# Full-height score products, a row tensor loaded by quarters, and a separate fine order of two streams for each engine

## The reference

```
q = (x @ Wq + bq).reshape(b, h, dh, t)        # likewise k, v; h = 16, dh = 8, t = 512
attn = jnp.einsum('bhdt,bhds->bhts', k, v) * temperature
attn = jax.nn.softmax(attn, axis=-1)
out = jnp.einsum('bhdt,bhts->bhds', q, attn)
...
h = shift_token(x)
q, k, v = jnp.split(h @ wqkv, 3, axis=-1)     # 8 heads of 64
q = l2norm(q) * qs ; k = l2norm(k) * ksc
q, k = rotary_xpos(q, k)                      # t*cos + rotate_half(t)*sin
x = x + local_attention(q, k, v) @ wo
h = layernorm(shift_token(x)) * lg + lb
a, g = split(h @ w1 + b1) ; x = x + (a * gelu(g)) @ w2 + b2
```

## Time and profile before

| | us |
|---|---|
| median of three executions | 1737.1 |
| profiled execution (its span) | 1743.6 (1741.7) |
| stage one with its start-up, to the last residual | 0 to 631 |
| stage two | 631 to 1741.7 |

### The profile page before, as it was taken

One profiled execution on the slowest core, in us unless ns is written; L12 is line 12 of the kernel. 1 busy time (PEld: TensorE's weight loads), 2 busy tenths in 40 slices (PEclk: granted clock), 3 DMA queues, 4 the chain that ended last, 5 costly groups with the idle time before them and its releaser, 6 DMA issues. The chain is left out here.

```text
span 1741.7 us, 21308 instructions
## 1 busy us (share of the span) xinstructions
PE 1380.9 (79%) x6968; PEld 733.4 (42%) x6968; DVE 1046.6 (60%) x2065; ACT 955.9 (55%) x2810; POOL 506.9 (29%) x525
## 2 busy tenths in 40 slices
PE   3898999989998976677686687687766877777876
PEld 3333333333332325445454454364444554544544
DVE  6665655666566666555556646657556566556563
ACT  0575655666576754555555465464555654545654
POOL 2000000000000024453443533624534525336241
PEclk9555555565555568898888898988988988889889
DMA  6212020211202000000011000010000010100010
GB/s 212 80 69 95 3 97 1 97 50 48 97 0 97 1 1 22 10 13 22 1 28 28 1 22 22 1 29 19 9 22 7 16 28 1 28 22 1 22 28 7
DMA packets 24157, 58.98 MB, mean 34 GB/s; under 512 B 2352, under 2 KB 2544, under 8 KB 22896
## 3 DMA queue, kind: packets, MB, share of 16 engines
q1 hardware_dynamic: 24048, 57.62, 10.9%
HBM read 23.98 MB, written 18.87 MB: 25 GB/s over the span
## 5 line engine op out<-in xcount | busy, mean ns | idle before, releaser
L530 ACT ACTIVATE E<-slot,neg_max 128x512 f32<-128x512 f32 x512 | 345.2, 686 | 229.7 <-DVE neg_max L804 125.8
L804 DVE TENSOR_REDUCE neg_max<-slot 128x2 f32<-128x1024 f32 x256 | 308.4, 1213 | 135.2 <-PE slot L1061 135.0
L1061 PE MATMUL slot<-v_rows,k_rows 32*128 32x512 f32 x512 | 269.3, 671 | 59.0 <-ACT E L530 47.3
L466 POOL TENSOR_TENSOR rot_work<-rot_work,rz 128x512 f32<-128x512 f32 x128 | 135.0, 1055 | 545.1 <-DVE rz L881 545.1
L589 ACT ACTIVATE rot_work<-bank,neg 128x128 f32<-128x128 f32 x512 | 180.8, 366 | 190.1 <-issue 119.0
L1061 PEld LDWEIGHTS slot<-v_rows,k_rows 32*128 32x128 f32 x512 | 132.1, 306 | 309.8 <-issue 174.6
L1071 PE MATMUL o_bank<-E,qz 128*32 128x512 f32 x1024 | 241.0, 1035 | 0.2 <-POOL qz L438 0.2
L1111 PE MATMUL bank<-wqkv_sb,hs 128*128 128x512 f32 x384 | 212.7, 670 | 14.3 <-ACT hs L556 13.6
L438 POOL TENSOR_TENSOR qz<-qT,rz 128x32 f32<-128x32 f32 x128 | 30.6, 239 | 586.3 <-DVE rz L808 586.3
L453 POOL TENSOR_TENSOR work<-work,rot_work 128x512 f32<-128x512 f32 x128 | 162.5, 1270 | 39.3 <-DVE rot_work L843 34.3
L1130 PEld LDWEIGHTS bank<-kT,q_bd 128*128 128x128 f32 x1024 | 142.1, 201 | 33.3 <-issue 28.7
(11 more groups left out here) (124 smaller groups left out, 1989.8 us busy)
## 6 DMA issues: line engine op xcount, KB each, us to landing
k_rows<-k_scr SPq DMA_DIRECT2D x8, 1024.0 KB, 5.7
v_rows<-v_scr SPq DMA_DIRECT2D x8, 1024.0 KB, 7.9
work<-v_al SPq DMA_DIRECT2D x16, 512.0 KB, 4.4
work<-v_al SPq DMA_DIRECT2D x16, 384.0 KB, 5.7
k_scr<-hi SPq DMA_DIRECT2D x16, 256.0 KB, 3.0
k_scr<-lo SPq DMA_DIRECT2D x16, 256.0 KB, 3.4
v_scr<-hi SPq DMA_DIRECT2D x16, 256.0 KB, 3.1
v_scr<-lo SPq DMA_DIRECT2D x16, 256.0 KB, 3.4
```

Source lines behind the costliest of these rows:

```text
L466: pool.tensor_tensor(pr[s][:, u % PR_SLOTS], pr[s][:, u % PR_SLOTS], rz2[s][:, u, :].unsqueeze(2).broadcast_to([P, 4, 2 * W]), ALU.mult).t ...
L530: last = act.activation(E[:, g % E_RING, 2 * half + m, :], slot[:, m], ACT.Exp, bias=neg_max[:, n, m:m + 1], accum_out=z[:, n, m:m + 1])
L804: dve.tensor_reduce(neg_max[:, n, :], slot[:], AX.X, ALU.max, negate=True).then_inc(max_ready, 1)
L1061: last = pe.matmul(slot[:, m], k_rows[32 * hh:32 * hh + 32, par, q, P * j:P * (j + 1)], v_rows[32 * hh:32 * hh + 32, par, q, :], start=Tru ...
```

## The change

Stage one: the score products use all 128 rows. `k_rows` is now zeroed once by POOL and holds, for each group `hh`, a 128-row tile in which only the 32 rows of that group are written; all 128 rows of `v_rows` stream. The larger `k_rows` has one buffer instead of two, so it is loaded in quarters: SP issues the DMA of quarter `hh` once the maxima of the previous sample's steps of that quarter are done. Each of the two banks of a slot is given back by its own exponential, and each score product waits for its own bank. The split of the keys on DVE moves from step 11 to 13, that of the values from 13 to 17, the value projection from 13 to 15, two ACT pieces by one step. Samples 1 to 6 run in a hardware loop on every engine (before, all were written out), so that the waits compare with registers.

Stage two: the cosine of k moves from POOL to DVE and the ACT copy of k (L564) goes; the scaling of q moves from DVE to POOL. Steps are cut into finer pieces, and each engine merges the pieces of the two streams by its own string in a table `ORDER` (880 letters for PE alone, without a repeating body). The zeroing of `q_bd` moves to the end of stage one.

```diff
-PREP_AT = {"var": 1, "rsqrt": 2, "normal": 4, "xT": 6, "hT": 7, "qT": 9, "queries": 10, "k": 11, "v": 13}
+PREP_AT = {"var": 1, "rsqrt": 2, "normal": 4, "xT": 6, "hT": 8, "qT": 9, "queries": 11, "k": 11, "v": 15}
+SPLIT_AT = {"k": 13, "v": 17}
...
-HEAD, BODY = interleaved()
+ORDER = {
+    "PE": (
+        "yxyyyyyxyyyxyyyyxxxxxxyyxyxyyyyyyyyxxyyyyyyyyyyxxyyyyxyyxxyyxyyxyxxxxyxxxyxxxxxxyxxyxyyyxyyxyxxxxyxx"
...
+def merge(streams, order):
+    for c in order:
+        next(streams["xy".index(c)])
...
-            k_rows = sa("k_rows", [P, 2, HQ, T], F32R)
+            k_rows = sa("k_rows", [P, HQ, HQ, T], F32R)
...
-                for scr, dst in ((k_scr, k_rows), (v_scr, v_rows)):
-                    sp.dma_start(dst[:, par].bitcast(F32),
-                                 scr[:].rearrange("q h t d s -> (h t d) q s")).then_inc(rows_in, 16)
+                sp.dma_start(v_rows[:, par].bitcast(F32),
+                             v_scr[:].rearrange("q h t d s -> (h t d) q s")).then_inc(v_in, 16)
+                for hh in range(HQ):
+                    if not (isinstance(b, int) and b == 0):
+                        sp.wait_ge(max_ready, b * STEPS - STEPS + (hh + 1) * (STEPS // HQ))
+                    sp.dma_start(k_rows[32 * hh:32 * hh + 32, hh].bitcast(F32),
+                                 k_scr[:, hh].rearrange("q t d s -> (t d) q s")).then_inc(k_in[hh], 16)
...
+            pool.memset(k_rows[:].bitcast(F32), 0.0).then_inc(k_zero, 1)
...
                 for m in range(2):
-                    last = act.activation(E[:, g % E_RING, 2 * half + m, :], slot[:, m], ACT.Exp,
-                                          bias=neg_max[:, n, m:m + 1], accum_out=z[:, n, m:m + 1])
-                last.then_inc(free, 1)
+                    act.activation(E[:, g % E_RING, 2 * half + m, :], slot[:, m], ACT.Exp,
+                                   bias=neg_max[:, n, m:m + 1], accum_out=z[:, n, m:m + 1]).then_inc(free, 1)
...
                     q = 2 * half + m
-                    last = pe.matmul(slot[:, m], k_rows[32 * hh:32 * hh + 32, par, q, P * j:P * (j + 1)],
-                                     v_rows[32 * hh:32 * hh + 32, par, q, :], start=True, stop=True)
-                last.then_inc(full, 1)
+                    bank = a_take(pe, b, n, m)
+                    last = pe.matmul(bank, k_rows[:, hh, q, P * j:P * (j + 1)], v_rows[:, par, q, :],
+                                     start=True, stop=True)
+                last.then_inc(a_full[n % SLOTS], 1)
...
             def b_rotary(s, k, l, n):
                 i, w = divmod(n, 2)
-                if w:
-                    done = (k * L + l) * J + i + 1
-                    pool.wait_ge(k_copied[s], done)
-                    v = qk[s][:, i, 1].rearrange("p (h d) -> p h d", h=H)
-                    pool.tensor_tensor(v, v, rot[:, l, i, 1, 0, :].unsqueeze(1).broadcast_to([P, H, DH]),
-                                       ALU.mult).then_inc(k_cos[s], 1)
-                    pool.wait_ge(k_cos[s], done)
...
-            for i in range((B - 2) // 2):
+            with dve.Fori(0, (B - 2) // 2) as i:
...
-                if w:
-                    dve.wait_ge(k_copied[s], (k * L + l) * J + i + 1)
-                    bank, free = b_see(dve, s, k, ("k", l, i))
-                else:
-                    dve.wait_ge(sq_ready[s], (k * L + l) * 2 * J + n + 1)
-                    bank, free = b_see(dve, s, k, ("q", l, i))
-                    dve.tensor_tensor(qk[s][:, i, 0, :].rearrange("p (h d) -> p h d", h=H),
-                                      bank[:].rearrange("p (h d) -> p h d", h=H),
-                                      rot[:, l, i, 0, 0, :].unsqueeze(1).broadcast_to([P, H, DH]), ALU.mult)
+                dve.wait_ge(sq_ready[s], (k * L + l) * 2 * J + n + 1)
+                bank, free = b_see(dve, s, k, ("qk"[w], l, i))
+                dve.tensor_tensor(qk[s][:, i, w, :].rearrange("p (h d) -> p h d", h=H),
+                                  bank[:].rearrange("p (h d) -> p h d", h=H),
+                                  rot[:, l, i, w, 0, :].unsqueeze(1).broadcast_to([P, H, DH]), ALU.mult)
```

More of the change, by code:

```diff
@@ L78 @@
 B_PER = [len(range(k, len(B_USES), B_BANKS)) for k in range(B_BANKS)]
[L81 to L95, removed]
@@ L98, in interleaved @@
[L98 to L114, removed]
@@ L482, in _ @@
             a_batch(0, 0)
-            for i in range((B - 2) // 2):
+            with pool.Fori(0, (B - 2) // 2) as i:
                 a_batch(2 * i + 1, 1)
@@ L488, in _ @@
             a_over(pool)
-            for step in HEAD:
-                b_step(0, 0, *step)
-            for k in range(B // STREAMS - 1):
-                for s, ahead, step in BODY:
-                    b_step(s, k + ahead if ahead else k, *step)
-            for s, ahead, step in BODY:
-                if not ahead:
-                    b_step(s, B // STREAMS - 1, *step)
+            for s in range(STREAMS):
+                pool.memset(q_bd[s][:], 0.0).then_inc(s_qbd, 1)
+            streams = [b_stream(s) for s in range(STREAMS)]
+            merge(streams, ORDER["POOL"])
         @block.scalar
@@ L653, in _ @@
             a_batch(0, 0)
-            for i in range((B - 2) // 2):
+            with act.Fori(0, (B - 2) // 2) as i:
                 a_batch(2 * i + 1, 1)
@@ L659, in _ @@
             a_over(act)
-            for step in HEAD:
-                b_step(0, 0, *step)
-            for k in range(B // STREAMS - 1):
-                for s, ahead, step in BODY:
-                    b_step(s, k + ahead if ahead else k, *step)
-            for s, ahead, step in BODY:
-                if not ahead:
-                    b_step(s, B // STREAMS - 1, *step)
+            streams = [b_stream(s) for s in range(STREAMS)]
+            merge(streams, ORDER["ACT"])
         @block.vector
@@ L1007, in _ @@
                 s_link(dve.memset(hs[s][W:P, 0:1], 0.0))
-            for step in HEAD:
-                b_step(0, 0, *step)
-            for k in range(B // STREAMS - 1):
-                for s, ahead, step in BODY:
-                    b_step(s, k + ahead if ahead else k, *step)
-            for s, ahead, step in BODY:
-                if not ahead:
-                    b_step(s, B // STREAMS - 1, *step)
+            streams = [b_stream(s) for s in range(STREAMS)]
+            merge(streams, ORDER["DVE"])
         @block.tensor
@@ L1235, in _ @@
             a_batch(0, 0, first=True)
-            for i in range((B - 2) // 2):
+            with pe.Fori(0, (B - 2) // 2) as i:
                 a_batch(2 * i + 1, 1)
```

416 lines of the change are left out of this document (243 added, 173 removed).

## The result

The changed kernel takes 1353.0 us (median of four executions, 1350.7 to 1358.7); the kernel before took 1740.3 us beside it on the same chip. The ratio is 0.7777, with a 95% interval of 0.7737 to 0.7817. The forecast was 1368 us, in a range of 1280 to 1535.

The account below looks back on a forecast made before the run. Stage one was taken as bound by PE at a low clock, stage two by waits in fixed engine orders. 1743.6 - 182 - 187 = 1375, less 6.5 for the median: 1368 us, range 1280 to 1535 (chance 0.80).

Parts of the forecast that it names:

- The clock: Stage one: with all products using 128 rows, PE's granted clock rises from 0.52 to 0.95 or more.
- rival by which busy time alone decides: Stage one: fuller products leave the clock low, only stalls shrink, 20 us gained, 1530 us in all; chance 0.11.
- The price of a 128-row product: Stage one's score products: 128 rows cost 0 extra at one clock, with bounds of 0 to +0.24 us a pair.
- A middle sample: Stage one, six samples between first and last: 74.4 us each go to 50.5, bounds 47 and 58; -144 us.
- The pauses of DVE: Stage one: DVE's splits, residual with normalisation and variance empty ACT, adding 5 us a sample.
- slack of 0.8 us in the slots: Stage one's three PSUM slots: a DVE pause longer than 3 x 1.33 - 3.2 = 0.8 us empties ACT.
- First and last sample: Stage one: the first goes from 79.6 to 50.5 us (-29), the last from 55.4 to about 46 (-9).
- The later splits: Stage one: splitting two steps later removes DVE's 6.94 us wait for the key projection; without the cover 6 us come back.
- The quarters: Stage one: loading `k_rows` by quarters costs 0, with 6 us left for the quarter issued behind `v_rows`.
- Stage two: New orders cut PE's idle time from 283 to 146 us, the clock gives -50: -187 us in sum.
- the cover: Stage two: other PE work between transpose groups covers about 3.9 of the 5.8 us wait out of the norm, -62 us.
- The moved work: Stage two: DVE -24 us but not the bound; POOL's serial scaling 11.7 us, 5.8 more in a stream's chain.

Follow-up runs that it names:

- runs with 32, 64 and 128 rows: The changed kernel (128 rows, 1353.0 us) against the same with score products cut to 32 rows (1464.2 us) or 64 rows (1414.2 us).
- 32-row run: The changed kernel with score products cut back to the 32 rows that hold data: 1464.2 us.
- whole-slot run: The changed kernel, but each PSUM slot is given back whole after both exponentials and both score products wait for it: 1351.8 us.
- run with the old order: The changed kernel with stage two merged by the one common list of before, the moved work kept: 1581.2 us, stage two 1115.2.
- run with the old division and the new orders: The changed kernel with its fine orders, but ACT copying k, POOL doing its cosine and DVE scaling q as before: 1412.3 us.
- stage two alone: The kernel before with only stage two changed (orders and work), stage one as before: 1503.7 us, ratio 0.866.

## Why the prediction was right, step by step

**The clock** was the largest step in stage one, and held: 0.95 forecast "or more", 0.95 measured. The reading behind it, that the mixture with 32-row products holds the clock down and that zeros in the weights don't, is what the runs with 32, 64 and 128 rows show. The rival by which busy time alone decides is out: the 32-row run is 98% busy at 0.53.

**The price of a 128-row product** was taken as nothing; a score product is now recorded with 0.49 to 0.51 us. But the first of a run is recorded with 0.49 us at the full clock with 32 rows too. Where two stand back to back at the full clock, the second starts 0.33 us after the first with 32 rows (at 516.58 in the kernel before) and 0.34 us after it with 128 rows (at 187.38). So the number stands. The reason given for it did not hold: the 1.99 us for four of the earlier trace rows are records of fp32 products at the full clock, set beside fp32r products at half the clock. Choosing 0 from bounds of 0 to 0.24 us (0.23 by its own terms) was luck.

**A middle sample** was to take 50.5 us and takes 52.7. ACT is busy 45.3 us (46.3 in the earlier trace rows, which the sum used), and it idles 7.2 us, not 5. The pauses of DVE were the right mechanism, since taking 2 us of its work away gave 1.25 us a sample, but all stalls together were priced some 2 us too low; at most 0.5 of it are the loops. That a slack of 0.8 us in the slots sets how much of a pause comes through is not shown: the whole-slot run takes 0.34 us of it away, and the times don't tell the two kernels apart. PE is busy 45.2 us a sample and not 43; the preparation at half clock was 70.4 - 61.9 = 8.5 us, and more by the prediction's own terms, which have it as 7.2.

**First and last sample**: -24 instead of -29 for the first (its clock is 0.89), -12.5 instead of -9 for the last, since ACT needs only 38.7 us there (38.9 in the earlier trace rows, so "about 46" was misread). Stage one in sum: -168, forecast -182.

**The later splits** do what was said: without them the prediction had 6 us a sample come back, 42 for seven samples, and the run gave 39. **The quarters** cost nothing: no wait of PE for `v_rows` or `k_rows` appears in the trace. From the page's DMA issues (KB each, us to landing):

```profile
v_rows<-v_scr SPq DMA_DIRECT2D x8, 1024.0 KB, 6.4
k_rows<-k_scr SPq DMA_DIRECT2D x32, 256.0 KB, 7.5
```

**Stage two** was to lose 187 us and lost 226. By place, forecast and measured: out of the norm -62 and -78, into it -20 and -36, probabilities -35 and -61, the rest -20 and -2, so PE's idle time went to 106 us and not 146. (The 77 us of the rest were too many: 206 us of the earlier trace rows, without the ends of the stage, were taken from 283 us of the whole stage; over the whole, the three places have 213.) The clock was to give 50 us, and PE's busy time fell by 48. The step that was mis-sized is the cover: I took a wait as covered only by the work between two groups in PE's own order, and the waits shrank by more, likely because the other engines' own orders also bring the awaited result earlier. The table above shows that the orders carry 168 to 230 us, but no run changed one engine's order alone, so this cause is argued and not shown.

**The moved work** was costed at nothing for its share of DVE and at up to 46 us for the serial scaling. POOL's scaling takes 1057 ns, not the 1455 of the earlier trace rows:

```profile
L472 POOL TENSOR_TENSOR work<-work,rn 128x512 f32<-128x512 f32 x128 | 132.2, 1057 | 26.3 <-DVE rn L791 26.3
```

In the run with the old order it is 1047 ns, so it was not the order that made it shorter. The run with the old division and the new orders shows what did, since there some of POOL's scalings of k stand beside DVE's of q (first two rows) and some alone (last two):

```profile
834.49 5.04 DVE L900 TENSOR_TENSOR work<-work,rn 128x512 f32<-128x512 f32 x4
834.53 4.44 POOL L479 TENSOR_TENSOR work<-work,rn 128x512 f32<-128x512 f32 x3 [3.03 <-DVE rn L801]
...
760.75 2.50 DVE L900 TENSOR_TENSOR work<-work,rn 128x512 f32<-128x512 f32 x4
...
770.26 1.04 POOL L479 TENSOR_TENSOR work<-work,rn 128x512 f32<-128x512 f32 x1
```

Of POOL's 64 scalings there, 31 stand apart from DVE's and take 1.04 us; the 33 beside them take 1.51 on average. DVE's take 0.69 us where none of POOL's is under way when they start and 1.53 where one is, so the 1.07 of the earlier trace rows is a mean of two kinds. The second to start ends a fixed time after the first: one of POOL's ends 0.90 us after DVE's has ended (56 of 64 in the kernel before, all within 3 ns), one of DVE's 0.55 us after POOL's (32 of 64). The Trainium skill (SBUF — State Buffer, section SBUF: two separate sides) says that DVE and GpSimd share a pair of ports which an instruction holds for itself; these rows agree: the second comes to its end only after the first has ended, and always by the same time. The serial row is 8 x 1.06 = 8.5 us, then, not 11.7. DVE's busy time in stage two fell by 10 us and not by the 24 forecast; 5 of the missing 14 are the next point.

**The zeroing of `q_bd`** was given no price, and it has one. At the end of stage one POOL is at it from 463.18 us for 6.96 us, and DVE's second small step of stage two, a copy of 128x4 elements that takes 0.17 us elsewhere, ends only when POOL has ended:

```profile
463.18 6.96 POOL L510 MEMSET q_bd<- 128x4096 f32 x2 [2.66 <-DVE x_sb L845]
...
465.08 5.09 DVE L782 COPY var<-stats 128x4 f32<-128x4 f32 x1
```

It takes 5.08 or 5.09 us in all eleven kernels that zero `q_bd` there, and 0.17 in the kernel before and in that with stage two alone, which zero it at the start of the program. The stage two of the latter is also 7.7 us shorter than that of the changed kernel. So some 5 us of stage two are likely the price of the move. `q_bd` now lies in the space that stage one's buffers give up, so it can't be zeroed much earlier; another engine or a later place was not tried.

**The rivals.** The one of the low clock would have ended elsewhere than I wrote: I gave the schedule 20 us at 1.2 GHz, and it gives 45 there; with the 39 us that stage two gave beyond its forecast, that case is 1464 us and not 1530. The step that failed in it is "only stage one's stalls shrink, 76 to about 73": a middle sample at 32 rows takes 68.7 us (74.4 before) with PE 98% busy, so most of the 6.2 us that PE idled in a sample were to be had. The forecast came out 15 us above the result because errors offset each other: 14 us too much taken off in stage one, 39 too little in stage two, and 6.5 us taken off for the median, which now stands 2.4 us above the profiled execution (1350.65 us). The chance of the range, 0.80, comes to 0.78 by the prediction's own terms.

## What to carry to other kernels

A product that uses few rows of the array can hold the clock of all products around it down, even with PE 98% busy; filling the rows with zero weights cost no time of its own here and brought the other half of the clock. When an engine waits in the middle of its order, look at what is queued behind it: two waits of DVE that grew by some 26 us together cost 39, since maxima stood behind them, ACT behind those and PE behind ACT. The new division of work was worth nothing under the order made for the old one and 61 us under its own, so the two are to be changed and judged together; and when three engines are level, even a slower engine with idle time can take work from them and win. Two elementwise instructions with both operands in SBUF, one on DVE and one on POOL, were no parallel work here: ask what a piece costs alone before moving it.

## What the hardware showed that was not expected

The clock does not switch with the number of rows but shifts in share: 0.53, 0.68 and 0.95 with 32, 64 and 128 rows in the score products, at 98, 94 and 86% busy time. A scaling of a 128x512 tile takes 1.04 us on POOL and 0.69 us on DVE alone. Beside each other both take about 1.5 us: whichever starts second ends a fixed time (0.90 or 0.55 us) after the first has ended.
